# RWKV attention and expert FFN with post layer norm: the output projection of all batches but the first in three fp32r terms, and some halves and mixes moved

## The reference

```
key, value, rec = hidden*mix + shifted*(1-mix)          # three mixes, shifted by one token
k = key @ Wk;  v = value @ Wv;  r = sigmoid(rec @ Wr)
rwkv = scan over tokens of exp-weighted k and v (numerator / denominator)
x = layernorm(hidden + (r * rwkv) @ Wo)
h = x @ down (8 experts x 16), router logits = x @ router_w
gate = softmax(logits), only its top 2;  out = layernorm(x + (silu(h) * gate) @ up)
```

## Time and profile before

| | us |
|---|---|
| median of 3 runs | 481.06 |
| the profiled execution | 481.16 |
| its span, first to last instruction | 479.0 |
| PE busy | 459.9 |
| DVE busy | 413.5 |
| ACT busy | 351.5 |
| POOL busy | 289.0 |

### The profile page before, as it was taken

One profiled execution on the slowest core, in us unless ns is written; L12 is line 12 of the kernel. 1 busy time (PEld: TensorE's weight loads), 2 busy tenths in 40 slices (PEclk: granted clock), 3 DMA queues, 4 the chain that ended last, 5 costly groups with the idle time before them and its releaser, 6 DMA issues. The chain is left out here.

```text
span 479.0 us, 6524 instructions
## 1 busy us (share of the span) xinstructions
PE 459.9 (96%) x1930; PEld 329.7 (69%) x1930; DVE 413.5 (86%) x620; ACT 351.5 (73%) x792; POOL 289.0 (60%) x279
## 2 busy tenths in 40 slices
PE   8999899999999999999999999999999999999993
PEld 3444557776788777878778777887778775777461
DVE  6998979697989979998799988999799987785676
ACT  1677665765788698876888788876888868647675
POOL 2454784667647888369846688269864693321315
PEclk9999899999999999999999999999999999999998
DMA  8503320022000042001320042100420042300015
GB/s 251 191 1 119 95 74 1 19 92 89 1 1 0 2 141 95 29 0 61 117 89 0 1 132 70 64 0 23 134 88 22 1 133 90 131 0 1 0 45 219
DMA packets 20675, 31.41 MB, mean 66 GB/s; under 512 B 2080, under 2 KB 7200, under 8 KB 20640
## 3 DMA queue, kind: packets, MB, share of 16 engines
q1 hardware_dynamic: 20640, 31.00, 19.8%
HBM read 22.60 MB, written 8.39 MB: 65 GB/s over the span
## 5 line engine op out<-in xcount | busy, mean ns | idle before, releaser
L554 ACT ACTIVATE PR<-PR 128x512 f32<-128x512 f32 x128 | 74.3, 580 | 39.0 <-DVE PR L836 16.9
L1119 POOL TENSOR_SCALAR NM<-SUM,RS 128x1 f32<-128x1 f32 x30 | 8.1, 271 | 121.5 <-ACT RS L554 121.4
L1113 POOL TENSOR_TENSOR DQ<-DEN,EX 128x512 f32<-128x512 f32 x32 | 41.3, 1291 | 32.3 <-DVE DEN L807 32.3
L861 DVE SCALAR_TENSOR_TENSOR KT<-D,VEC,XT 128x512 f32<-128x512 f32 x57 | 54.0, 983 | 2.6 <-POOL KL L1097 2.6
L317 PE MATMUL PV<-VH,WVH 128*128 128x512 f32 x112 | 49.3, 441 | 2.1 <-DVE NU L831 2.0
L321 PE MATMUL PR<-RL,WRH 128*128 128x512 f32 x112 | 45.5, 407 | 3.2 <-POOL RL L1097 3.2
L317 PE MATMUL PK<-KH,WKH 128*128 128x512 f32 x112 | 48.5, 433 | 0.0
L807 DVE TENSOR_TENSOR_SCAN DEN<-PK,EX 128x512 f32<-128x512 f32 x32 | 39.0, 1220 | 9.9 <-ACT EX L554 7.5
L317 PE MATMUL PR<-RH,WRH 128*128 128x512 f32 x112 | 44.3, 395 | 0.6 <-DVE RW L848 0.6
L321 PE MATMUL PV<-VL,WVH 128*128 128x512 f32 x112 | 44.7, 399 | 0.0
L318 PE MATMUL PV<-VH,WVL 128*128 128x512 f32 x112 | 44.4, 396 | 0.0
(11 more groups left out here) (227 smaller groups left out, 1257.3 us busy)
## 6 DMA issues: line engine op xcount, KB each, us to landing
XT<-in_xt SPq DMA_DIRECT2D x32, 256.0 KB, 3.4
XN<-in_x SPq DMA_DIRECT2D x28, 256.0 KB, 2.6
out<-XN SPq DMA_DIRECT2D x28, 256.0 KB, 2.0
X1T<-in_wo SPq DMA_DIRECT2D x1, 1024.0 KB, 5.1
KT<-in_wo SPq DMA_DIRECT2D x4, 256.0 KB, 2.7
XT<-in_x SPq DMA_DIRECT2D x4, 256.0 KB, 4.4
out<-XT SPq DMA_DIRECT2D x4, 256.0 KB, 2.4
X1T<-in_wk SPq DMA_DIRECT2D x2, 256.0 KB, 5.0
```

The lines of the kernel that those rows point to most:

```text
L554: eng.activation(*a, **k).then_inc(q[s], 1)
L861: eng.scalar_tensor_tensor(out=full(b, which, c), in0=D[:, c, :], scalar=VEC[:, 2 + which, c:c + 1], in1=XT[:, c, 0:T], op0=ALU.mult, op1= ...
L1113: eng.tensor_tensor(DQ[:, :], DEN[:, 0:T], EX[:, 1, :], ALU.add).then_inc(q["e"], 1)
L1119: eng.tensor_scalar(NM1[:, col(t)], total, RS1[:, col(t)], scale, ALU.mult, ALU.mult)\
```

## The change

Six things change.

1. Slot 4: PE projects tile 0 ahead of `rec(4)` and no longer behind it.
2. The first two chunks of VH and VL are made at the end of the third slot of a batch (ACT, POOL) instead of in the fourth. On POOL they stand ahead of the next denominator.
3. In the fourth slot from batch 1 on DVE makes the first receptance mix ahead of the gate and of the next slot's scan, and the last one ahead of `weigh`.
4. POOL makes the last block of WRL behind the KL of slot 6.
5. Batch 6 is projected with TH and TL like batches 1 to 5, its TH and TL being made in slots 27 to 29.
6. Batch 7 is projected in three terms from KH and KL, which are free by then: `last_highs` on ACT and `last_lows` on POOL fill them chunk by chunk from RW, and PE does the products with the highs of three chunks of tiles 28 to 30, then the lows, then the fourth chunk; an up-projection (tile 20) and all of tile 31 follow before the turn of tile 28. Wo is no longer loaded into KT.

```diff
--- before.py
+++ after.py
@@ -176,7 +176,7 @@
 
-        FIRST, SPLIT = NT, NT * (LAST - 1)
+        FIRST, SPLIT = NT, NT * LAST
 
@@ -270,10 +270,6 @@
             for b in range(1, LAST):
-                if b == LAST - 1:
-                    for c in range(C):
-                        eng.wait_ge(q["lo"], 3 * C * (LAST - 1) + C + c + 1)
-                        eng.dma_start(KT[:, c, :], wo[128 * c:128 * c + 128, :]).then_inc(q["wot"], 16)
                 if b >= 2:
@@ -339,11 +335,14 @@
 
-            def projected(t, chunks):
-                b, n = divmod(t, NT)
+            def by_high(t, chunks, high):
                 for c in chunks:
-                    last = eng.matmul(projected_at(t), RW[:, rw_at(C * b + c), 128 * n:128 * n + 128],
-                                      (X1T if b == 0 else KT)[:, c, :], start=(c == 0), stop=(c == C - 1))
+                    eng.matmul(projected_at(t), high(c), WOH[:, c, :], start=(c == 0), stop=False)
+                    eng.matmul(projected_at(t), high(c), WOL[:, c, :], start=False, stop=False)
+
+            def by_low(t, chunks, low):
+                for c in chunks:
+                    last = eng.matmul(projected_at(t), low(c), WOH[:, c, :], start=False, stop=(c == C - 1))
                 return last
@@ -351,33 +350,30 @@
                 else:
-                    eng.wait_ge(q["res"], t - (b == LAST - 1 and n == 1))
+                    eng.wait_ge(q["res"], t - (b == LAST - 1 and n > 0))
                 if b == LAST - 1 and n == 1:
                     eng.wait_ge(q["res2"], NT * (LAST - 2))
-                if FIRST <= t < SPLIT:
-                    if t == FIRST:
-                        eng.wait_ge(q["woh"], 1)
-                        eng.wait_ge(q["wol"], 1)
-                        eng.wait_ge(q["wol1"], 1)
-                    eng.wait_ge(q["th"], halved(t + 1))
+                if t < FIRST:
+                    if n == 0:
+                        eng.wait_ge(q["rw"], C * (b + 1))
                     for c in range(C):
-                        i = half_at(b, c)
-                        eng.matmul(PP[:, :], TH[:, i, :], WOH[:, c, :], start=(c == 0), stop=False)
-                        eng.matmul(PP[:, :], TH[:, i, :], WOL[:, c, :], start=False, stop=False)
-                    eng.wait_ge(q["tl"], halved(t + 1))
-                    for c in range(C):
-                        last = eng.matmul(PP[:, :], TL[:, half_at(b, c), :], WOH[:, c, :], start=False, stop=(c == C - 1))
+                        last = eng.matmul(projected_at(t), RW[:, rw_at(C * b + c), 128 * n:128 * n + 128], X1T[:, c, :],
+                                          start=(c == 0), stop=(c == C - 1))
                     last.then_inc(q["wo_"], 1)
                     return
-                if n == 0:
-                    eng.wait_ge(q["rw"], C * (b + 1))
-                if t == SPLIT:
-                    eng.wait_ge(q["wot"], 16 * C)
-                projected(t, range(C)).then_inc(q["wo_"], 1)
-
-            def project_most(t):
+                if t == FIRST:
+                    eng.wait_ge(q["wol"], 1)
+                    eng.wait_ge(q["wol1"], 1)
+                eng.wait_ge(q["th"], halved(t + 1))
+                by_high(t, range(C), lambda c: TH[:, half_at(b, c), :])
+                eng.wait_ge(q["tl"], halved(t + 1))
+                by_low(t, range(C), lambda c: TL[:, half_at(b, c), :]).then_inc(q["wo_"], 1)
+
+            def tokens(t):
+                return slice(128 * (t % NT), 128 * (t % NT) + 128)
+
+            def project_high(t):
                 n = t % NT
-                eng.wait_ge(q["rw"], U - 1)
                 if n == 0:
@@ -386,11 +382,18 @@
                     eng.wait_ge(q["hc"], NT * LAST)
-                projected(t, range(C - 1))
+                eng.wait_ge(q["rh"], C - 1)
+                by_high(t, range(C - 1), lambda c: KH[:, c, tokens(t)])
+
+            def project_low(t):
+                eng.wait_ge(q["rl7"], C - 1)
+                by_low(t, range(C - 1), lambda c: KL[:, c, tokens(t)])
 
             def project_rest(t):
-                eng.wait_ge(q["rw"], U)
-                projected(t, range(C - 1, C)).then_inc(q["wo_"], 1)
+                eng.wait_ge(q["rh"], C)
+                by_high(t, range(C - 1, C), lambda c: KH[:, c, tokens(t)])
+                eng.wait_ge(q["rl7"], C)
+                by_low(t, range(C - 1, C), lambda c: KL[:, c, tokens(t)]).then_inc(q["wo_"], 1)
 
@@ -483,10 +486,12 @@
                     key(s + 1)
+                if s == C:
+                    project(0)
                 rec(s)
...
                     ffn_up(t3 + 3)
-                if j == 0:
+                if j == 0 and b > 1:
                     for t in now[:1]:
@@ -515,17 +520,18 @@
             hidden(t6 + 3)
-            project_most(t7)
-            project_most(t7 + 1)
-            project_rest(t7)
-            project_rest(t7 + 1)
-            project_most(t7 + 2)
-            project_rest(t7 + 2)
+            for t in range(t7, t7 + 3):
+                project_high(t)
+            for t in range(t7, t7 + 3):
+                project_low(t)
+            for t in range(t7, t7 + 3):
+                project_rest(t)
+            ffn_up(t5)
+            project_high(t7 + 3)
+            project_low(t7 + 3)
+            project_rest(t7 + 3)
             turn(t7)
             ffn_turn(LAST - 1)
-            ffn_up(t5)
-            project_most(t7 + 3)
-            project_rest(t7 + 3)
             turn(t7 + 1)
@@ -647,6 +653,12 @@
 
+            def last_highs(*chunks):
+                for c in chunks:
+                    eng.wait_ge(q["k"], U)
+                    eng.wait_ge(q["rw"], C * LAST + c + 1)
+                    act("rh", KH[:, c, :], RW[:, rw_at(C * LAST + c), :], ACT.Copy)
+
             def hidden_copy(t):
@@ -693,6 +705,8 @@
                 k = gated(s)
+                for t in now[:1] if s == U - 3 else []:
+                    halve(t)
                 for t in past[1:]:
@@ -702,11 +716,13 @@
                 if j == 3 and batch(b + 1):
-                    highs(b + 1, 1)
+                    highs(b + 1, 1, range(2, C))
                 if k is not None and s < U - 1:
...
                     ffn_out(b - 2)
+                if s == U - 1:
+                    last_highs(2)
                 receptance(s)
@@ -714,14 +730,16 @@
                     highs(b + 1, 2, range(2))
-                if 2 * C <= s < C * LAST:
+                if 8 <= s < C * LAST:
                     log_g(s)
                     factor(s)
+                for t in now[1:]:
+                    halve(t)
                 if s < U - 1:
...
                     highs(1, 0, range(C - 1, C))
-                if not 2 * C <= s < C * LAST:
+                if not 8 <= s < C * LAST:
                     log_g(s)
@@ -732,7 +750,7 @@
                     high_weights(2)
-                for t in now[:1] if j == 3 and b < LAST - 1 else []:
+                for t in now[:1] if j == 3 and b < LAST else []:
                     halve(t + 1)
@@ -742,6 +760,8 @@
                     halve(t + 1)
+                if j == 2 and batch(b + 1):
+                    highs(b + 1, 1, range(2))
                 if s == C:
@@ -755,8 +775,10 @@
                 if s == U - 2:
+                    last_highs(0, 1)
                     ffn_out(b - 2)
             t5, t6, t7 = (NT * (LAST - i) for i in (2, 1, 0))
+            last_highs(3)
             ffn_in(LAST - 1)
@@ -1002,7 +1024,9 @@
                     mixes(b + 1, 0, 3)
-                if 2 * C <= s < C * LAST:
+                if j == 3 and b:
+                    mixes(b + 1, 2, 0)
+                if 8 <= s < C * LAST:
                     gate(s)
@@ -1014,15 +1038,15 @@
                 if j == 3 and b:
-                    mixes(b + 1, 2, 0, 1)
-                if not 2 * C <= s < C * LAST:
+                    mixes(b + 1, 2, 1)
+                if not 8 <= s < C * LAST:
                     gate(s)
...
                 if j == 3:
-                    mixes(b + 1, 2, *((2,) if b else (0, 1, 2)))
+                    mixes(b + 1, 2, *((2, 3) if b else (0, 1, 2)))
                 if s == U - 1:
@@ -1041,7 +1065,8 @@
                 if j == 3:
-                    mixes(b + 1, 2, 3)
+                    if b == 0:
+                        mixes(b + 1, 2, 3)
                     if s < U - 1 and batch(b - 2):
@@ -1106,6 +1131,12 @@
 
+            def last_lows(*chunks):
+                for c in chunks:
+                    eng.wait_ge(q["rh"], c + 1)
+                    eng.tensor_tensor(KL[:, c, :], RW[:, rw_at(C * LAST + c), :], KH[:, c, :].bitcast(F32), ALU.subtract)\
+                       .then_inc(q["rl7"], 1)
+
             def denominator(u):
@@ -1149,9 +1180,13 @@
                 denominator(s)
+                for t in now[:1] if s == U - 3 else []:
+                    low_of_tile(t)
                 for t in past[1:]:
                     normalise(t)
-                if C <= s < 2 * C - 1:
```

(16 more changed lines are left out.)

## The result

| | before | changed |
|---|---|---|
| median of the runs, us | 481.28 (480.91 to 482.7) | 473.38 (473.06 to 473.77) |
| ratio | | 0.983 [0.981, 0.985] |
| profiled execution, its span | 481.16, 479.0 | 473.77, 471.9 |

Faster by 7.9 us, where 4.15 was forecast.

What follows compares the result with a forecast made beforehand. The prediction took the loop of DVE, ACT and POOL, not PE, to set the period in batches 2 to 5. Terms 0 - 2.5 + 0.75 - 2.4 = -4.15 took 481.16 to 477.0 us, own range 475.2 to 478.6.

Steps and rivals of the forecast that it cites:

- Term A: Slot 3 to slot 7: later POOL start (+1.15) and WRL taken away (-1.26) cancel; 0, between -0.3 and +1.1 us.
- Term B: Slot 7 to slot 9: early mixes bring slot 8's denominator scan forward; -2.5 us, between -1.65 and -3.0.
- the second rival: Batch 2: PE's r(8) becomes the new wait and batch 1's gain is lost, 479.5 us; 0.27 together with a lost tail gain.
- Term C: Slot 9 to slot 28, five fourth slots: +0.15 us a batch, +0.75 in all (-0.25 to +2).
- Term D: Slot 28 to the end: batches 6 and 7 in three fp32r terms shorten the tail; -2.4 us (-0.7 to -3.5).
- The signs named in advance: Wrong if the period of batches 2 to 5 moves by more than 0.4 us, or the tail isn't 1.5 to 3.5 shorter.
- PE is the bound: Whole kernel: PE time taken off comes back whole, 12 us, giving 469; chance 0.03.
- the rival: Slots 11 to 27: mix 1 waits behind a full POOL instruction, RH 1 ends 1.2 us late, total 483.1; chance 0.10.

Runs made afterwards that it cites:

- the run with both parts: Kernel before with only the first projection moved ahead of rec(4) and the last WRL moved behind the four KL: 480.20 us, ratio 0.997.
- mixes alone: Kernel before with only receptance mix 0 ahead of the gate and mix 3 ahead of the weighing in fourth slots: 477.29 us, ratio 0.992.
- the mixes moved: Changed kernel with receptance mix 0 at the end of the third slot and mix 1 in its place ahead of the gate: 467.44 us, ratio 0.971.
- with it inside: Changed kernel with receptance mixes 0 and 1 both ahead of the gate in the fourth slot: 474.82 us, ratio 0.985.

## Why the prediction was wrong

The direction was right. All four terms came out lower than they were put, so that nothing evened out. Two of them failed in kind: in A the two halves didn't cancel, and C, put as a loss, is a gain. B and D were mis-sized, and stand near the forecast partly by luck.

*Term A, "cancel ... Sum at slot 7: 0".* This failed most plainly. The gain of the WRL was sized right (1.26 against 1.28). The delay that it was to cancel, +1.1, reached DVE's queue in full in the run with both parts, but it arrives at slot 5's scan as 0.57, since the KT mixes behind it then run in 2.07 us in place of 2.65. In the changed kernel nothing of it arrives, because the value halves in slot 2 had brought slot 4's scan 0.9 ahead (without the halves slot 5's scan is 0.53 late again); the prediction put nothing there. A small net gain of two large terms is only as good as the weaker one.

*Term B, -2.5.* The better end, -3.0, was nearer: the scan of slot 8 came 3.25 earlier by mixes alone. Mix 3's part was 2.1 (1.65 put; 1.95 with all of ACT's wait), mix 0's 1.06, as worked out. 0.42 is given back at slot 9 to PE, the wait that the second rival named, but with a sixth of its price. By luck this give-back, which the sum didn't have, hides more than half of the 0.75 by which the scan of slot 8 was missed.

*Term C, +0.75.* Gate and RH 1 came where they were forecast (1.7 late; 223.28, at the better end of 223.3 to 223.75). The step that failed is the price of mix 3 ahead of the weighing: 0.14 was put for the copies that no longer wait, 0.28 a slot was measured with that edit alone. The 0.14 is ACT's idle time before the fourth copy. The two copies together took 1.41 in the kernel before:

```profile
225.82 1.41 ACT L554 ACTIVATE RH<-D 128x512 fp32r<-128x512 f32 x2
```

In the changed kernel they take 1.16 (the row at 222.48 above), 0.25 less: copies that don't wait begin 0.51 apart though each is shown with 0.64, and this overlap was lost with the wait too. And the up to 0.45 put for a mix 1 behind a POOL instruction never fell due in the changed kernel. Five slots at -0.37 against the forecast are 1.85 of the 3.95 missed; A is 1.4, B 0.3, D 0.4.

*Term D, -2.4.* Near in sum, wrong in its parts. Batch 6 was read from one wait of slot 30, 1.3; there were two, and it gave 1.9. Batch 7 was put at 1.1 and gave 0.9. The turn of tile 28 behind tile 31 was counted only as something that eats up gain; with the old order 1.5 of the gain is gone.

*The signs named in advance.* Of the two by which the prediction would call itself wrong, neither came: the period of a batch moved by 0.2, not by 0.4, and the tail is 2.8 shorter, within 1.5 to 3.5. A bound of 0.4 on something that counts five times was too wide to catch a miss of 1.85.

*Against the rivals.* That PE is the bound was held at 0.03 for the changed kernel, rightly; but it was argued from waits alone. The runs put a number on it: with the mixes moved, the same PE work of a batch fits into 53.61 us, so before there were at least 1.6 us of slack in each 55.25. PE's busy share of 96% hid it: it is shown busy for 54.46 us a batch in the changed kernel (mean of two batches), more than the 53.61 in which the same matmuls were then done, so part of what is shown as busy there isn't work. My expectation for the moved mix took this busy time as a floor and was wrong by it.

## What to carry to other kernels

Count what an instruction costs where it stands, not what it costs alone: one mix took 0.74 us beside an idle POOL and 1.78 beside a busy one, and with it out of the full slot C was -8.7 us, in place of -0.2 with it inside and all else the same. When ACT waits for DVE in each period, look for a stretch in which POOL is idle, before changing the order inside the full one. Read what a wait costs from the distance between the instructions that follow, not from the idle time alone. Don't take the busy time of PE as a floor; and where two terms of a sum cancel, test or bound each by itself.

## What the runs showed of the hardware

A mix (two operands in SBUF) and a POOL instruction that are due together don't slow each other evenly: one keeps its own time and the other ends later, by about 0.5 us where the first is short and by 1.0 where it is long. For the normalising and mix 1 it is 0.79 and 1.30 (POOL first), or 1.28 and 0.78 (DVE first); for the denominator and mix 0 in slot 15, 1.28 and 1.78, where the mix ends 0.55 behind the denominator, as it ended 0.55 behind the VL in the earlier trace rows. A start 0.1 us earlier was enough to be the first at 106.57 in the changed kernel, where the denominator is stretched from 1.28:

```profile
106.57 0.75 DVE L883 SCALAR_TENSOR_TENSOR D<-D,VEC,XT 128x512 f32<-128x512 f32 x1
106.67 1.77 POOL L1144 TENSOR_TENSOR DQ<-DEN,EX 128x512 f32<-128x512 f32 x1
```

The Trainium skill, "SBUF — State Buffer", § SBUF: two separate sides, says so: of the two, the one that starts first has the shared ports for its whole instruction. The trace agrees in who keeps its time at 0.1 us between the starts; what the denominator loses, 0.49, is somewhat less than the 0.65 that was left of the mix when it was due. It holds for the normalising too, which has one tensor operand only; in the prediction I had taken that single operand as a reason against the rival.

Nearer together, the rows don't tell who will be first: the normalising's row begins 0.03 to 0.06 before mix 1's in the three slots that it won and 0.02 to 0.04 before it in the seven that it lost, and the same stretch of program lost 0.5 us in three slots of five or in none. So two kernels that differ only in their tail differed by 1.4 us in the middle, and the first scan of slot 0 stood between 0.04 before and 1.14 us behind 17.15 in kernels with the same instructions up to it. So a difference of about 1.5 us between two traces means little without the terms between fixed rows.
